# Clearing the padding rows of two sorted token tables chunk by chunk in the attention stages, on one Trainium2 core

## What is computed

```python
x = layernorm(x + attn0(x))        # 16 heads of running sums of exponentials
x = layernorm(x + moe0(x))         # one of 8 experts per token, ReLU, times its probability
x = layernorm(x + attn1(x))        # softmax attention, 16 heads of 8, position bias
x = layernorm(x + moe1(x))         # shared SwiGLU + one of 8 SwiGLU experts per token
```

## Time and profile before

| | |
|---|---|
| median of three runs | 2504.85 us (2502.02 to 2507.4) |
| span of the profiled execution | 2581.7 us (the page gives no other time of that execution) |
| attention_one | 0 to about 719 us, DVE busiest |
| stage b | 727 to 841 us |
| attention_two | 843 to 2286 us, PE (TensorE) busiest |
| stage d | 2290 to 2440 us |
| finish | to the end |

### The profile page before, as it was taken

How to read it: one execution, slowest core, us unless ns; L and a number is a source line. 1 busy time by engine, 2 the same in 40 slices (tenths; PEclk the granted TensorE clock), 3 DMA queues, 4 the chain that set the end, 5 groups by cost and what they waited for, 6 DMA issues and landing times. The chain is left out here.

```text
span 2581.7 us, 49760 instructions
## 1 busy us (share of the span) xinstructions
PE 2096.5 (81%) x14284; PEld 1360.5 (53%) x14284; DVE 1814.2 (70%) x5026; ACT 1562.8 (61%) x3460; POOL 773.2 (30%) x612
## 2 busy tenths in 40 slices
PE   7576767677659299989999989899998899949886
PEld 5355555545637155555555555555555555526553
DVE  6799898989821277777778767777777678733366
ACT  3544545454324188877888778788887788812221
POOL 5555655655600112212211221122112210000066
PEclk9778778787879599999999999899999999979999
DMA  2330000000046222112201220122022101034332
GB/s 79 118 118 24 26 28 24 24 24 25 29 157 197 74 58 62 36 38 67 62 23 50 67 58 28 51 66 58 18 61 66 49 26 53 10 110 161 134 97 87
DMA packets 83431, 164.16 MB, mean 64 GB/s; under 512 B 11428, under 2 KB 39076, under 8 KB 80884
## 3 DMA queue, kind: packets, MB, share of 16 engines
q1 hardware_dynamic: 73844, 142.35, 17.5%
q0 software_dynamic: 8192, 16.79, 2.0%
q10 hardware_dynamic: 1152, 2.10, 0.2%
HBM read 110.23 MB, written 58.31 MB: 65 GB/s over the span
## 5 line engine op out<-in xcount | busy, mean ns | idle before, releaser
L1581 DVE CUSTOM_DVE_ANT_0 c_sums<-c_s,bias 128x512 f32<-128x512 f32 x1024 | 673.9, 687 | 200.6 <-PE c_s L1319 154.5
L1469 ACT ACTIVATE c_sums<-c_sums,c_low 128x512 f32<-128x512 f32 x1024 | 733.1, 739 | 39.0 <-DVE c_low L1581 27.9
L1328 PE MATMUL c_turned<-ident,c_sums 128*128 128x128 f32 x4096 | 656.1, 284 | 66.2 <-ACT c_pT L1176 31.5
L1328 PEld LDWEIGHTS c_turned<-ident,c_sums 128*128 128x128 f32 x4096 | 513.8, 146 | 229.3 <-ACT c_pT L1176 85.9
L1176 ACT COPY c_pT<-c_turned 128x512 f32<-128x512 f32 x768 | 454.5, 592 | 181.7 <-PE c_turned L1328 167.0
L1319 PE MATMUL c_s<-c_kst,c_qst 72*128 72x512 bf16 x1024 | 408.9, 400 | 45.6 <-DMA c_qst<-parts_d 27.2
L1341 PE MATMUL c_o<-c_pT,c_vst 128*32 128x256 f32 x4096 | 334.5, 399 | 0.7 <-ACT c_pT L1176 0.7
L1176 DVE COPY c_pT<-c_turned 128x512 f32<-128x512 f32 x256 | 176.7, 690 | 147.6 <-PE c_turned L1328 141.3
L501 ACT ACTIVATE v<-a_bank,dg 128x64 f32<-128x64 f32 x1024 | 217.2, 378 | 28.5 <-DVE q L697 14.9
L1268 POOL TENSOR_TENSOR c_rstd<-c_ve,minus_half 128x4 f32<-128x4 f32 x32 | 33.1, 1034 | 656.9 <-DVE c_ve L122 656.9
L1319 PEld LDWEIGHTS c_s<-c_kst,c_qst 72*128 72x128 bf16 x1024 | 104.6, 102 | 236.9 <-issue 146.9
(11 more groups left out here) (254 smaller groups left out, 2894.8 us busy)
## 6 DMA issues: line engine op xcount, KB each, us to landing
c_kst<-parts_d SPq DMA_DIRECT2D x48, 384.0 KB
c_qst<-parts_d SPq DMA_DIRECT2D x48, 384.0 KB
parts_d<-c_parts SPq DMA_DIRECT2D x32, 384.0 KB
d_w<-in_wd SPq DMA_DIRECT2D x24, 384.0 KB, 3.1
b_w<-in_wb SPq DMA_DIRECT2D x24, 321.0 KB, 3.4
bias_d<-line_d SPq DMA_DIRECT2D x16, 448.0 KB
bias<-bias_d SPq DMA_DIRECT2D x1, 7168.0 KB, 21.9
b_x<-xs_d SPq DMA_DIRECT2D x24, 256.0 KB, 2.6
```

The lines of the kernel that those rows point to most:

```text
L1328: mm = nc.tensor.transpose(pT_ps[n % 2][:, c, :], sums[n % BUFS][:, c * P:(c + 1) * P], keep.ident[:])
L1469: nc.scalar.activation(sums[b][:], sums[b][:], ACT.Exp, bias=low[b][:], scale=-1.0).then_inc(sem("exp_done"), 1)
L1581: v.tensor_tensor_reduce(sums[n % BUFS][:], s_ps[n % BANKS][:], bias, 1.0, 3.0e38, ALU.add, ALU.min, low[n % BUFS][:]).then_inc(sem("low_r ...
```

## The change

Both kinds of fill leave the expert stages. A new input `zeros` of 128 x 512 floats lies in HBM. In batch b of the attention stage, SP issues one DMA within HBM that clears rows 512·b to 512·b + 511 of all 8 regions (2 MB), and once per stage one that clears the spare rows. POOL waits for the clearing of chunk b ahead of its indirect writes of batch b. SP waits for all of them at the end of the stage.

```diff
+def clear_rows(eng, name, b, io, done):
+    regions = io[name][0:SPARE, :].rearrange("(e r) w -> e r w", e=E)
+    eng.dma_start(regions[:, bass.ds(GROUP * b, GROUP), :].rearrange("e (p t) w -> p e (t w)", t=T),
+                  io["zeros"].unsqueeze(1).to_broadcast([P, E, T * W])).then_inc(done, 16)
+
+def clear_spare(eng, name, io, done):
+    eng.dma_start(io[name][bass.ds(SPARE, GROUP), :].rearrange("(p t) w -> p (t w)", t=T), io["zeros"]).then_inc(done, 16)
...
@@ attention_one, SP
                     if on[1]:
                         load(s)
+                        clear_rows(sp, "xs_d", s.b, io, sem("rows_clear"))
...
+                clear_spare(sp, "xs_d", io, sem("spare_clear"))
                 loop(sp, step, first=0)
+                sp.wait_ge(sem("spare_clear"), 16)
+                sp.wait_ge(sem("rows_clear"), 16 * NB)
...
@@ attention_one, POOL, route_scatter
                     pool.wait_ge(sem("slot_ready"), s.b + 1)
+                    pool.wait_ge(sem("rows_clear"), 16 * (s.b + 1))
...
@@ experts
-        zeros = sb("zeros", [P, T, W])
-        fill = sb("fill", [P, E], I32)
-        def fill_behind(eng, experts):
-            eng.wait_ge(sem("zeros_ready"), 1)
-            eng.wait_ge(sem("fill_ready"), 1)
-            for e in experts:
-                r = which(eng, fill, e, SPARE - GROUP)
-                eng.dma_start(rows_of(src, r), zeros[:]).then_inc(sem("fill_out"), 16)
...
-                fill_behind(sp, range(0, E, 2))
-                sp.dma_start(rows_of(src, SPARE), zeros[:]).then_inc(sem("fill_out"), 16)
...
-                        if isinstance(s.b, int) and s.b == 0:
-                            sp.wait_ge(sem("fill_out"), 16 * E + 16)
...
-                nc.gpsimd.memset(zeros[:], 0.0).then_inc(sem("zeros_ready"), 1)
...
-                v.tensor_copy(fill[:], keep.run[:]).then_inc(sem("fill_ready"), 1)
...
-                fill_behind(act, range(1, E, 2))
...
@@ attention_two, SP
                 def body(s, tail=True, front=True):
+                    clear_rows(sp, "zs_d", s.b, io, sem("rows_clear"))
                     if front:
                         stack(s.ahead())
...
                 load(at(1))
+                clear_spare(sp, "zs_d", io, sem("spare_clear"))
                 body(at(0), tail=False)
...
+                sp.wait_ge(sem("spare_clear"), 16)
+                sp.wait_ge(sem("rows_clear"), 16 * NB)
...
@@ _layout
+    out["zeros"] = np.zeros((P, T * W), f)
```

## The result

The changed kernel takes 2493.7 us (median of 14 runs, 2489.78 to 2499.72), the kernel before 2504.63 us (14 runs, 2498.23 to 2507.4). The ratio is 0.9959 [0.995, 0.9968]: by it the kernel is 10.3 us faster (8.0 to 12.5). The forecast was 2498.0 us in a range of 2493 to 2507, and "faster" at 0.62. The profiled execution of the changed kernel took 2497.3 us, with a span of 2495.5 us.

The account below looks back on a forecast made before the run. No engine bounds the whole kernel; the first loads of rows set the starts of stages b and d. Gains of 3.6 + 3.5 = 7.1 us, scaled to 6.9, with clearings costing nothing, gave 2498.0 us, range 2493 to 2507.

Parts of the forecast that it names:

- The starts of b and d: Expert stages b and d: without the fills the first load of rows goes out 3.6 and 3.5 us sooner.
- The far end of the bounds: Starts of b and d: 7.9 us gained together if the value loads take 0.26 us both times.
- That span is 3.1% above the median of the runs: Whole kernel: the 7.1 us gain scaled from the profiled span of 2581.7 us to the runs' measure, 6.9 us.
- The clearing at 315 GB/s: Each 2.10 MB clearing in the attention stages takes 6.7 us at the hardware queue's rate, with 12.9 us kept as slow case.
- Attention_one, steady and first steps: Clearings there cost nothing: in steady steps SP's next transfer is 12.9 us later; in first steps later landings are not waited for.
- the `xT` then lands near 154: Attention_one's third step: `xT` queues behind clearing, bias load and store, landing near 154 but used near 174.
- The start of attention_two: Clearing of chunk 0 beside the first stacks delays the first scores by nothing to 5.5 us; taken as nothing.
- The bodies: Attention_two, bodies 1 to 15: clearings behind the store cost nothing, since SP next issues at 1083.07.
- rival 2: Clearings hold up instruction packets, in attention_two for example; at 1 us per clearing 25 us slower, 2530; chance 0.10.
- Bodies should keep their 85 and 89 us by turns: Sign in attention_two: unchanged body lengths; longer ones with idle time ended by "issue" on PE, ACT or DVE mean rival 2.
- The sum: Whole kernel: 3.6 + 3.5 = 7.1 us of the profiled span, 6.9 us in the runs' measure, giving 2498.0 us.

Follow-up runs that it names:

- e1: The kernel before, unchanged, profiled once more: 2504.23 us, with a profile span of 2503.1 us.
- e2: Kernel before with the clearings added to the attention stages and the fills of the expert stages kept: ratio to before 1.0006.
- e3: Changed kernel, but only the first 3072 rows of each region cleared, all in attention_one's steps 0, 1 and 15: ratio to before 0.9995.
- e5: Changed kernel with chunk 0 of zs_d and the spare rows cleared behind the stacks of batch 1: 2494.09 us, ratio to before 0.9963.
- e4: Changed kernel with a second 2 MB transfer behind each clearing, into a table of its own: ratio to before 0.9972.
- e8: Changed kernel with both tables cleared in attention_one and nothing cleared in attention_two: ratio to before 0.9966.
- e10: Changed kernel with stage b's plan held back by eight POOL memsets, on chip C: 2591.42 us, ratio to before 1.0027.
- e12: Changed kernel with both tables cleared in attention_one and nothing in attention_two, measured again: ratio to before 0.9967.
- e7: Kernel before with the change for zs_d and stage d alone, xs_d still filled in stage b, on chip C: ratio to before 1.0041.

## Why the prediction came out as it did

- **The starts of b and d** ("3.6 + 3.5 = 7.1 us"): right in place and kind, small by 0.7 us. Measured 4.0 and 3.8, and within 0.2 of that in every profile that has the change, for b on chips A, B and D, for d on all four. The missing memset was worth what was taken, `row` is complete 0.5 us sooner in b. The value loads were sized too high: the first one of `b_row` takes 0.27 us, not the 0.8 taken from a row whose values run from 260 to 1000 ns. Load, register work and release are 0.78 us together, where 1.3 and 1.05 were taken. The far end of the bounds, 7.9 us, is nearly what came (7.8).
- **"That span is 3.1% above the median of the runs, so in their measure 7.1 x 2504.85 / 2581.7"**: wrong in kind. The 3.1% were not spread over the execution. They all lay in the bodies of attention_two (e1), so the starts of b and d needed no scaling. The slip was worth 0.2 us here; in a case where the gain sat in those bodies it would have mattered.
- **The clearing at 315 GB/s, 6.7 us**: right. It takes a little over 7 us in attention_one, with 392 GB/s in its best window beside whatever else was in flight.
- **Attention_one, steady and first steps, nothing**: right (e2, and 718.4 for 718.2). The bias load lands 7.3 us later where 6.7 were forecast, and "the `xT` then lands near 154" came out at 142.09 + 13.2 = 155.3; its users wait no longer than before. What had not been foreseen is that SP itself is held, 6.58 us in one issue, where the prediction had the transfer waiting in the queue and SP free. e2, with the same clearing in that step, has 6.51 us there, and e3, without it, 0.35 us. That the queue was full is the likely reason; no view shows it.
- **The start of attention_two, between nothing and 5.5 us, for which the prediction took nothing**: some 0.4 us (e5). The windows of the changed kernel show most of the clearing through by about 880, 11 us behind its issue, then the stacks' tail alone, and from 889.6 on, when `qst` has landed, the same small share once more:

```profile
875.00:880.00 5.00, 0.00 (x0) 0.00 (x0) 0.00 (x0) 0.00 (x0) 0.00 (x0) 0.50 0.89 355
880.00:885.00 5.00, 0.00 (x0) 0.00 (x0) 0.00 (x0) 0.00 (x0) 0.00 (x0) 0.50 0.20 85
885.00:889.00 4.00, 0.00 (x0) 0.00 (x0) 0.00 (x0) 0.00 (x0) 0.00 (x0) 0.50 0.17 72
891.00:893.00 2.00, 2.00 (x6) 0.60 (x5) 2.00 (x9) 1.82 (x3) 0.00 (x0) 0.50 0.20 77
895.00:897.00 2.00, 1.82 (x12) 1.15 (x11) 2.00 (x6) 1.93 (x5) 0.00 (x0) 0.92 0.01 5
```

  This fits thirteen engines that clear while three carry `qst`, with the three taking their share of the clearing behind it: the clearing of chunk 0 lands 26.4 us behind its issue at 869.36 (the page's 25.3 is the median over the clearings of `zs_d`), at 895.8, which is 6 us after the scores began. The prediction's estimate for such a share was 5.5 us; it came, but where nobody waits for it. The Trainium skill (DMA: Bandwidth & Descriptors, Queues, rings and completion order) says that an engine consumes the descriptors of a ring in order; by that rule the clearing's share costs `qst` nothing, and the trace agrees within those 0.4 us.
- **The bodies, "nothing", and rival 2** ("Bodies should keep their 85 and 89 us by turns"): on chips A, B and D the bodies take 79 us and 81 to 84 us by turns with or without the clearing, and at the price of 1 us a clearing rival 2 is out there (e2, e4, e8). On chip C the kernels with the clearing were slower than before, by what comes to 0.7 to 0.9 us a body, and had more stalls. The stalls are ended by "remote", not by "issue" as the rival had it. That they are late instruction packets is not shown, nor that they are the loss (e10). The prediction had the first kind of stall in the trace that it read, in 12 bodies, and passed over it, since it asked only for idle time ended by "issue".
- **The sum.** Starts 7.8, start of attention_two −0.4, which leaves 7.4 us. Three measurements give 10.3, 8.3 and 8.5, with intervals from 5 to 12.5; two of the intervals hold 7.4, that of the first (8.0 to 12.5) doesn't. One to three us of gain beyond the starts are thus possible and unexplained. The means of run clocks are 0.9111 to 0.9116 for the changed kernel and 0.9095 to 0.9099 for before, but that tells little: the granted clock is 0.50 in the windows from 719 to 739 and from 2286 to 2302 of before, and 7.8 us at 0.50 taken out of 2504 us at 0.9098 leave a mean of 0.9111 by themselves. The bodies of the ten profiles on chips A, B and D and of the changed kernel on record spread over 1269.5 to 1278.4 us in no clear order of kernels. By the distance of the stores, the spread sits in the bodies where the loop turns back, 80.9 to 84.0 us; the others in the loop take 78.8 or 78.9 us in e1 and e2 and 79.1 or 79.2 in the rest. e8 and e12 speak against a gain from clearing in attention_two; e10 was to test the starts alone and didn't. The source of this gain stays open.

The forecast was on the right side because the two starts were found and sized; at 6.9 us it was under the 8.3 to 10.3 measured, and 2493.7 lies 0.7 us inside the lower end of the range. It was luck that the comparison on record had the pace of chips A, B and D: by e7 and e10 the change would rather lose on chip C. None of the kernels here beats the changed one beyond the intervals; e5 and e8 equal it.

## What to carry to other kernels

Work that an expert stage needs, but whose place doesn't depend on late data, can be put behind transfers of an earlier stage: ask what SP delivers next, how many us lie between, and which other engine's DMAs are in flight and waited for. Sixteen clearings cost nothing measurable on chips A, B and D with 5 us of spare cover at each, and six in a row beside indirect writes whose landing DVE waits for cost 5.2 us (e3). And before a profile is read, hold its span against the runs: a difference of 3% is a finding of its own, and a stage whose stalls are ended by something unnamed is where to look first when more DMA is added; on chip C there was a loss, though its place is not shown.

## What the runs showed of the hardware that was not expected

- **Two paces of one kernel.** The kernel before takes 2504 to 2505 us on three chips and 2584 on a fourth. Each chip was used once, so whether the pace belongs to the chip or to the occasion is not shown. Judged by its stalls and its span, the profile of before on record is of the second kind. Between it and that of e1 lie 5.6 us a body, a gap of PE of 2 us and 6 to 7 us at half clock behind it.
- **A short gap can cost more behind it than in itself.** PE was idle for 1.95 us, and the 1.2 GHz level that followed cost about another 3.5 us. The length of the gap alone does not set that. In the same profile PE's gap of 2.62 us where the loop turns back is followed by a granted clock of 0.50 from 1148 to 1150, of 0.74 to 1152 and of 1.00 from there on, and e10's gap of 1.35 us behind its second stall left the clock at 1.00.
- **Three engines carry a stack.** The tail of `qst` runs at a DMA share of 0.17 to 0.20 and 71 to 85 GB/s, with or without the clearing, and PE waits 27 to 28 us for it. The Trainium skill (DMA: Bandwidth & Descriptors, Why a DMA increments its semaphore by 16 and not by 1) says that a transfer uses the largest number of engines up to 16 that divides the slowest dimension of both sides. On the source side that dimension is 3 here (`[strides[1], PARTS]`), on the tile's side 24 rows, so 3 engines by that rule, and the trace agrees: 0.17 to 0.20 of 16 are 2.7 to 3.2. No run changed it.
- **Clearing within HBM is quick.** In bodies of attention_two the clearing and the stacks' other transfers reach 394 GB/s from 1011 to 1013 and 418 in the next window of the changed kernel, with PE busy throughout:

```profile
1013.00:1015.00 2.00, 2.00 (x20) 1.10 (x19) 1.54 (x13) 2.00 (x4) 0.00 (x0) 1.00 1.08 418
```
